# Attention scores in 24 units of one shape instead of 28 of three, with the products around them put in other places

## The reference

```python
    h = _L0_tok_ref(x, L0_tok_Wv, L0_tok_bv, L0_tok_Wo, L0_tok_bo, L0_tok_decay_w)
    h = h + _L0_attn_ref(_layernorm(h, axis=-1), L0_attn_wq, L0_attn_bq, L0_attn_wk, L0_attn_bk, L0_attn_wv, L0_attn_bv, L0_attn_wo, L0_attn_bo)
    h = h + _L0_ffn_ref(_layernorm(h, axis=-1), L0_ffn_router_w, L0_ffn_wg_r, L0_ffn_wu_r, L0_ffn_wd_r, L0_ffn_wg_s, L0_ffn_wu_s, L0_ffn_wd_s)
    return h
```

```python
        scores = jnp.einsum('bhqd,bhkd->bhqk', q, k) / jnp.sqrt(jnp.float32(hd))
        causal = jnp.tril(jnp.ones((s, s), dtype=bool))
        scores = jnp.where(causal, scores, -jnp.inf)
        weights = jax.nn.softmax(scores, axis=-1)
        attn = jnp.einsum('bhqk,bhkd->bhqd', weights, v)
```

## Time and profile before

| | |
|---|---|
| device time, median of 3 runs | 1868.26 us (1855.72 to 1869.14) |
| span of the profiled execution | 1852.8 us |
| lowest run over that span | 2.9 us |
| TensorE, VectorE, ScalarE, GpSimd busy | 1700.5, 1437.1, 976.7, 1056.0 us |
| a step of the attention phase | 34.09 us |

### The profile page before, as it was taken

The page is one execution under the profiler, slowest core; times in us unless marked ns, Lnnn a source line. Parts: engine busy times, 40 slices in busy tenths (PEclk is TensorE's granted clock), DMA queues, the critical chain, the costliest instruction groups (busy, mean ns, idle before and its releaser), DMA issues. The chain is left out here.

```text
span 1852.8 us, 49530 instructions
## 1 busy us (share of the span) xinstructions
PE 1700.5 (92%) x14718; PEld 1360.0 (73%) x14719; DVE 1437.1 (78%) x3985; ACT 976.7 (53%) x2048; POOL 1056.0 (57%) x1446
## 2 busy tenths in 40 slices
PE   5899999999999999999999998589999986988883
PEld 4677777777777777777777775368888876877773
DVE  4589899999999899899999996378888971455554
ACT  1166666666676666666666765333444422544441
POOL 4045555555555655655555556446777770567666
PEclk8899999999999999999999999679999997999996
DMA  2555556556556555555565453223333356999996
GB/s 76 80 132 152 141 128 158 142 119 166 141 135 144 147 147 138 135 154 142 123 162 141 123 147 99 109 74 105 126 120 120 122 155 169 286 327 326 323 331 220
DMA packets 226548, 291.13 MB, mean 157 GB/s; under 512 B 57142, under 2 KB 188954, under 8 KB 226458
## 3 DMA queue, kind: packets, MB, share of 16 engines
q1 hardware_dynamic: 190042, 186.14, 40.3%
q0 software_dynamic: 18048, 49.31, 8.2%
q10 hardware_dynamic: 18368, 54.64, 7.7%
HBM read 83.25 MB, written 129.69 MB: 115 GB/s over the span
## 5 line engine op out<-in xcount | busy, mean ns | idle before, releaser
L752 ACT ACTIVATE probs<-bank 128x376 f32<-128x376 f32 (+2 forms) x896 | 440.7, 529 | 272.9 <-PE bank L621 261.0
L843 DVE TENSOR_REDUCE neg_max<-bank 120x1 f32<-120x376 f32 (+2 forms) x896 | 507.0, 587 | 53.7 <-PE bank L587 49.7
L587 PE MATMUL bank<-k_rows,q_rows 64*128 64x128 f32 (+2 forms) x1536 | 403.7, 345 | 3.1 <-ACT probs L752 2.4
L621 PE MATMUL bank<-q_rows,k_rows 64*120 64x120 f32 (+2 forms) x1536 | 369.9, 336 | 3.9 <-ACT probs L752 3.6
L982 POOL TENSOR_SCALAR_AFFINE_SELECT probs<-probs 128x512 f32<-128x512 f32 (+1 forms) x384 | 232.4, 631 | 209.5 <-ACT probs L752 209.3
L604 PE MATMUL bank<-causal,own_row 56*120 56x56 bf16 (+4 forms) x1792 | 300.9, 248 | 8.7 <-DMA k_rows<-k_flat_hi 3.5
L587 PEld LDWEIGHTS bank<-k_rows,q_rows 64*128 64x128 f32 (+1 forms) x1536 | 246.2, 186 | 6.7 <-ACT probs L752 4.6
L2205 POOL DMA_INDIRECT y_got<-y_sorted,p_route x188 | 182.4, 970 | 119.7 <-issue 117.6
L621 PEld LDWEIGHTS bank<-q_rows,k_rows 64*128 64x128 f32 (+1 forms) x1536 | 229.8, 183 | 8.7 <-ACT probs L752 5.8
L604 PEld LDWEIGHTS bank<-causal,own_row 64*128 64x128 bf16 (+2 forms) x1792 | 153.4, 115 | 110.3 <-DVE neg_max L843 39.9
L1847 POOL DMA_INDIRECT x_sorted<-r_normed,route x188 | 184.3, 981 | 83.6 <-issue 59.0
(11 more groups left out here) (235 smaller groups left out, 4148.8 us busy)
## 6 DMA issues: line engine op xcount, KB each, us to landing
x_sorted<-zeros ACTq DMA_DIRECT2D x32, 816.0 KB, 3.8
y_sorted<-zeros ACTq DMA_DIRECT2D x32, 816.0 KB, 4.3
x_rows<-x_sorted SPq DMA_DIRECT2D x51, 512.0 KB, 6.4
y_sorted<-p_y_rows SPq DMA_DIRECT2D x51, 512.0 KB, 6.4
q_rows<-q_flat_hi SPq DMA_DIRECT2D x256, 94.0 KB
k_rows<-k_flat_hi SPq DMA_DIRECT2D x248, 94.0 KB
q_rows<-q_flat_lo SPq DMA_DIRECT2D x128, 94.0 KB
out_dram<-base SPq DMA_DIRECT2D x47, 256.0 KB, 5.0
```

The source lines that it names most:

```text
L587: last = eng.matmul(ps[0:T[t], m * w:(m + 1) * w], q[rows, slot, t * P:t * P + T[t]], k[rows, slot, 0:w], start=False, stop=(m == len(head ...
L621: last = eng.matmul(ps[0:T[t], m * w:(m + 1) * w], k[64 * c:64 * c + 64, slot, t * P:t * P + T[t]], q[64 * c:64 * c + 64, slot, t * P:S], ...
L752: eng.activation(probs[g % 2][0:T[t], first:first + len(heads), OFF[t]:OFF[t] + w], bank_exp[n % 2][0:T[t], 0:len(heads) * w].rearrange("k ...
L843: eng.tensor_reduce(dst, src, AX.X, ALU.max, negate=True).then_inc(max_taken, 1)
```

## The change

Each group has six units, so a step has 24. The first two (`PAIRS`) hold the second query tile of two heads each, for maxima and for exponents. The other four hold one head: for the maxima its third tile (376 keys) and behind it its first (128 keys), for the exponents its first (376 queries) and behind it its third (120). All banks are then nearly full, and all tiles are taken as 128 rows; for this `k_rows` is widened to 384 with zeros, and of `q_rows` the whole width is copied. A reduction of a one-head unit leaves four maxima, three of which belong to the third tile; `turn_maxima` joins these with one more reduction. `probs` is laid out anew (`OFF`), the masks come in the order second, first, third tile, and the first as well as the third wait for the group's last exponent.

What stands beside the units moves on all engines. TensorE: hid0 and hid1 after unit 1, value products of the last element's group 3 and val0 after 3, conv0 and conv1 after 7, nT after 9, value products of group 0 after 11, q0 and q1 after 13, k0 and k1 after 15, value products of group 1 and out0 after 17, those of group 2 and out1 after 21, val1 after 23. ScalarE's `keep` goes to units 4, 12, 18 and 22 (each behind that unit's exponent), the copies of conv to 7. SyncE's `load_x` moves to the head of the step.

The diff, cut to its core:

```diff
-    GROUPS, UNITS = 4, 7
+    GROUPS, UNITS = 4, 6
-    OFF = [0, CUT[0], CUT[0] + CUT[1]]
+    OFF = [0, CUT[0] + CUT[2], CUT[0]]
...
-        k_rows = [sb(f"k_rows{p}", [P, 8, S], F32R) for p in range(2)]
+        k_rows = [sb(f"k_rows{p}", [P, 8, SPAN], F32R) for p in range(2)]
...
-                return (["hid0", "hid1"] * front + ["val0"] * maxima
+                return (["hid0", "hid1"] * front + ["val0"] * maxima + ["conv0", "conv1"] * mix
                         + ["nT0", "nT1", "q0", "q1", "k0", "k1"] * front
-                        + ["out0", "out1"] * finish + ["conv0", "conv1"] * mix + ["val1"] * maxima)
+                        + ["out0", "out1"] * finish + ["val1"] * maxima)
...
+        PAIRS = 2
+        VALUES_AT = (3, 11, 17, 21)
 
         def max_bank(n):
 
-            return bank_max[1 if n == LAST_UNIT else n % 3]
+            return bank_max[n % 3]
...
+                    if u < PAIRS:
+                        slot, t, at = 4 * (g // 2) + 2 * u + m, 1, 2 * P * m
+                    else:
+                        slot, t, at = 4 * (g // 2) + u - PAIRS, (2, 0)[m], NT * P * m
+                    keys = min(S, (t + 1) * P)
+                    last = eng.matmul(ps[:, at:at + keys], q[rows, slot, t * P:(t + 1) * P], k[rows, slot, 0:keys],
+                                      start=False, stop=(m == 1), skip_group_check=True)
...
+                    if u < PAIRS:
+                        slot, t, at = 4 * (g // 2) + 2 * u + m, 1, CUT[1] * m
+                    else:
+                        slot, t, at = 4 * (g // 2) + u - PAIRS, (0, 2)[m], CUT[0] * m
+                    last = eng.matmul(ps[:, at:at + CUT[t]], k[64 * c:64 * c + 64, slot, t * P:(t + 1) * P],
                                       q[64 * c:64 * c + 64, slot, t * P:S],
+                                      start=(m == 0), stop=(m == 1), skip_group_check=True)
...
-                        if n in (1, 2) and st.front:
-                            hid_rows(st, n - 1)
-                        if u == 4:
+                        if n == 1 and st.front:
+                            hid_rows(st, 0)
+                            hid_rows(st, 1)
+                        if n in VALUES_AT:
+                            group = VALUES_AT.index(n) - 1
                             for t in range(NT):
-                                if g == 0 and st.finish:
+                                if group < 0 and st.finish:
                                     products_with_values(st, 3, -1, t)
-                                if g > 0 and st.attend:
-                                    products_with_values(st, g - 1, 0, t)
-                        if n == 7 and st.maxima:
+                                if group >= 0 and st.attend:
+                                    products_with_values(st, group, 0, t)
+                        if n == 3 and st.maxima:
                             values(st, 0)
+                        if n == 7 and st.mix:
+                            conv(st, 0)
+                            conv(st, 1)
...
-                        if n in (20, 22) and st.finish:
-                            out_rows_(st, (20, 22).index(n))
-                        if n in (24, 27) and st.mix:
-                            conv(st, (24, 27).index(n))
-                        if n == 27 and st.maxima:
+                        if n in (17, 21) and st.finish:
+                            out_rows_(st, (17, 21).index(n))
+                        if n == 23 and st.maxima:
                             values(st, 1)
...
+                    if u < PAIRS:
+                        dst = probs[g % 2][:, 2 * u:2 * u + 2, OFF[1]:OFF[1] + CUT[1]]
+                        src = bank_exp[n % 2][:, 0:2 * CUT[1]].rearrange("k (m w) -> k m w", m=2)
+                    else:
+                        dst = probs[g % 2][:, u - PAIRS, 0:CUT[0] + CUT[2]]
+                        src = bank_exp[n % 2][:, 0:CUT[0] + CUT[2]]
+                    eng.activation(dst, src, ACT.Exp).then_inc(exp_done, 1)
...
-                        if n == 5 and st.finish:
+                        if n == 4 and st.finish:
                             keep(st, 3, -1)
-                        if n == 7 and st.front:
+                        if n == 6 and st.front:
                             normalise(st)
...
+                        if st.mix and n == 7:
+                            for j in range(2):
+                                take_hi(st, f"conv{j}", mixed[0][:, j, :])
...
-                        if n in (11, 18) and st.attend:
-                            keep(st, (11, 18).index(n), 0)
+                        if n in (12, 18, 22) and st.attend:
+                            keep(st, (12, 18, 22).index(n), 0)
...
-                HALF_1_AT = {10: (0, 1), 12: (2,), 14: (3,), 16: (4,)}
-                HALF_0_AT = {21: (0,), 23: (1, 2), 25: (3,), 26: (4,)}
+                HALF_1_AT = {9: (0,), 11: (1,), 12: (2, 3), 13: (4,)}
+                HALF_0_AT = {20: (0,), 21: (1,), 22: (2, 3), 23: (4,)}
...
+                    if u < PAIRS:
+                        src = max_bank(n)[:, 0:4 * P].rearrange("q (m w) -> q m w", m=2)
+                        dst = neg_max[:, half, 4 * e + 2 * u:4 * e + 2 * u + 2, 4]
+                    else:
+                        src = max_bank(n)[:, 0:4 * P].rearrange("q (c w) -> q c w", c=4)
+                        dst = neg_max[:, half, 4 * e + u - PAIRS, 0:4]
                     eng.tensor_reduce(dst, src, AX.X, ALU.max, negate=True).then_inc(max_taken, 1)
...
+                    eng.tensor_reduce(neg_max[:, half, :, 5], neg_max[:, half, :, 0:3], AX.X, ALU.min).then_inc(max_joined, 1)
+                    eng.wait_ge(max_joined, done)
...
+                        if st.mix and n == 8:
+                            for j in range(2):
+                                take_lo(st, f"conv{j}", mixed[1][:, j, :], mixed[0][:, j, :])
...
-                    last_unit = (7, 3, 1)[t]
+                    last_unit = (UNITS, PAIRS, UNITS)[t]
...
-                            for t in reversed(range(NT)):
+                            for t in (1, 0, 2):
                                 mask(st, g, t)
...
                     if st.attend:
                         max_rows(st, 1, 0)
+                    if st.mix:
+                        load_x(st)
                     if isinstance(st.i, int) and st.real == B - 1:
...
                     if st.finish:
                         store(st)
-                    if st.mix:
-                        load_x(st)
```

More of the change, by code:

```diff
@@ L186, in attention_phase @@
         max_taken = sem("max_taken")
+        max_joined = sem("max_joined")
         max_hi = sem("max_hi")
@@ L595, in hide_later_keys @@
                     ps = max_bank(g * UNITS + u)
-                    t, heads = MAX_UNITS[u]
-                    w, d, m = KEYS_OF[t], T[t], len(heads)
                     rows = slice(64 * (g % 2), 64 * (g % 2) + 64)
+                    if u < PAIRS:
+                        blocks = ps[:, 0:4 * P].rearrange("q (m w) -> q m w", m=2)[:, :, P:2 * P]
+                    else:
+                        blocks = ps[:, 2 * P:4 * P].rearrange("q (m w) -> q m w", m=2)
                     for h in (1, 0):
[L601 to L604, removed]
+                        eng.matmul(blocks[:, :, 64 * h:P], own_row[rows, h, :], causal[rows, h, 0:2, 64 * h:P],
                                    start=(h == 1), stop=False, skip_group_check=True)
@@ L635, in scores @@
                         open_exp(st, g, u)
-                    for m in range(4):
-                        if st.maxima and m < len(MAX_UNITS[u][1]):
+                    for m in range(2):
+                        if st.maxima:
                             scores_for_max(st, g, u, m)
-                        if st.attend and m < len(EXP_UNITS[u][1]):
+                        if st.attend:
                             scores_for_exp(st, g, u, m)
@@ L800, in step @@
                                     eng.wait_ge(rows_loaded[(st.b + 1) % 2][h], st.turn(1, 208, 208))
-                        if st.front and n in (13, 15):
-                            j = (13, 15).index(n)
-                            take_hi(st, f"q{j}", q_flat[0][:, j, :], bias=bias_q[:, j:j + 1])
-                        if st.front and n == 17:
+                            for j in range(2):
+                                take_hi(st, f"q{j}", q_flat[0][:, j, :], bias=bias_q[:, j:j + 1])
+                        if st.front and n == 15:
                             for j in range(2):
                                 take_hi(st, f"k{j}", k_flat[0][:, j, :], bias=bias_k[:, j:j + 1])
-                        if st.mix and n in (25, 27):
-                            j = (25, 27).index(n)
-                            take_hi(st, f"conv{j}", mixed[0][:, j, :])
-                        if n == 25 and st.attend:
-                            keep(st, 2, 0)
                 run_steps(eng, step)
@@ L954, in step @@
```

(4 more changed lines are left out.)

112 lines of the change are left out of this document (43 added, 69 removed).

## The result

The changed kernel takes 2097.7 us (median of 4 runs, 2091.34 to 2104.16) against 1868.7 (1855.72 to 1869.77): 1.126 times as long, interval 1.121 to 1.131. The forecast was 1977, in a range up to 2045.

What follows compares the result with a forecast made beforehand. TensorE was taken to bound the step, VectorE 3 us behind. Own work 30.4 + long wait 4.1 + smaller waits 3.1 = 37.6 us against 34.1; thirty steps and two end steps add 109: 1977 us, range 1872 to 2045.

Steps and rivals of the forecast that it cites:

- The main wait: Group 2's value products wait for masks queued behind GpSimd's join and ScalarE's keep: 4.1 us in every step.
- (a) to (c): Smaller waits: unit 7 behind keep and exponents 1.35 us, transposes at unit 9 0.9, k behind q's bank 1.3.
- load_x costs nothing: At the head of SyncE's step, its wait for conv precedes that for q, so it holds nothing up.
- the clock: Rival: the clock falls in the new wait each step, value products cost 1.1 us more; 2036 us, chance 0.20.
- (a) to (d): All four smaller waits, the last being hid1 behind val1's late reading, 0.4 us; sum 3.95, taken at 3.1.
- half of the rest: Of the smaller waits, those for k and hid1 counted half, those at unit 7 and the transposes whole.
- Own work: TensorE's work per step without waits: 34.1 - 3.0 - 0.7 = 30.4 us, bounds 30.0 to 30.8.
- merged dense products: hid, conv and q each become one block and lose one tiling change on TensorE: 3 x 0.12 us.
- The ends of the phase: Two attention steps behind the thirty steady ones, without hid, q and k: some 2 us more each.
- long wait absent: Rival: group 2's masks come within TensorE's 3.2 us of work; step about 33.2 us, 1841 us, chance 0.08.
- Hidden, but only by the new wait: Transfers from q's second copy to next step's unit 0: 12.2 us of issues against 16 of TensorE, 11.9 without the wait.

Runs made afterwards that it cites:

- Masks ahead: Changed kernel with GpSimd's join of groups 0 and 1 behind the masks of group 2 instead of ahead of them: 1969.28 us, ratio 1.057.
- copy at 17: Changed kernel with ScalarE's copy (keep) of group 1 at unit 17 instead of unit 18: 1976.46 us, ratio 1.060.
- units only: Changed kernel's 24 units kept, everything between them unmerged and put back to about where it stood before the change: 1832.48 us, ratio 0.983.
- filler matmuls: Changed kernel plus twelve matmuls that nothing reads, between unit 21 and group 2's value products: 2032.01 us, ratio 1.089.
- both ends: Changed kernel with group 2's masks ahead of the join and group 1's copy at unit 17 together: 1997.8 us, ratio 1.069.

## Why the prediction was wrong

**Right.** The main wait, to a tenth: 4.1 walked, 4.22 found, with the walk's 7.3 us from the products of group 1 to those of group 2 measured at 7.54 (575.11 to 582.65). Masks ahead, copy at 17 and units only show the cause. It has two parts, though, only one of which the text named: by masks ahead, 2.84 hangs on the masks behind the join, and 1.38 stays in units 18 to 21 without it. Runs of two units without a wait take 0.91 to 0.92, as said. The signs and places of (a) to (c) are right too, and load_x costs nothing.

**The step that failed: the clock.** It was put aside as a rival at 0.20, though the text itself counted about 14 matmuls in 3.41 us of the new wait, fewer than the 18 in the stretch where the trace of before shows the fall. It came in every step. It was also priced too low: 1.1, for value products alone, as the earlier trace rows show them. The lower level lasts on through out1 and into units 22 and 23, and the rows make it 2.07; filler matmuls give back 2.1. By the Trainium skill (TensorE: Matmul & The Clock Gate, section Why this matters for your kernels), which the text cited, gaps between bursts send the clock down. The trace agrees, with 0.50 behind a stretch that had 0.49 us of work in 3.75.

**Terms that were mis-sized.** (a) to (d) were taken at 3.1, "half of the rest" on the argument that one wait covers another. The small waits measured are 1.39, 0.96, 1.14 and 0.38, 3.87 in sum, where the walks had said 1.35, 0.9, 1.3 and 0.4. (a) to (c) stand each at its own place, and none covered another. The fourth agrees by luck: hid1 has no wait for the reading of val1. The 0.38 stands ahead of unit 1, whose scores wait for the exponent of the last unit of the step before, and that stands in ScalarE's queue behind the copy of group 2. The same place one step on:

```profile
588.61 0.58 ACT L736 ACTIVATE attn_of_odd<-bank,strip_half 128x376 f32<-128x376 f32 x1
589.07 1.80 ACT L753 ACTIVATE probs<-bank 128x496 f32<-128x496 f32 x3
589.27 0.34 PE L597 MATMUL bank<-causal,own_row 64*128 64x128 bf16 x2
589.72 0.38 PE L616 MATMUL bank<-q_rows,k_rows 64*128 64x248 f32 x1
...
591.55 0.28 PE L507 MATMUL bank<-w_mix_hi,mixed_lo 128*128 128x256 f32 x1
591.66 0.28 PE L507 MATMUL bank<-w_mix_hi,mixed_hi 128*120 128x256 f32 x1
```

The first exponent of the three at 589.07 is the last unit's, 589.72 begins unit 1's scores, and 591.66 is hid1, right behind hid0.

Own work was taken at 30.4 and is 30.8, the upper bound: of the 0.7 for merged dense products and value products beside them 0.3 came. By the starts of the blocks the pairs gave their part: hid takes 2.32 for 1.61 + 0.90, q 2.27 for 1.23 + 1.23, conv 1.73 for 0.96 + 0.79. Value products beside a dense block gave nothing: they take 1.40, and val0 and out0 beside them 1.62 each, as before with scores between (1.40, 1.62, 1.61). By the Trainium skill (TensorEngine Tiling (Array Packing), section Key Properties) a change from one tiling mode to another drains the engine, and products with values beside a dense block still make one. That fits these starts, though no run here shows the drain itself. The sum: 37.6 forecast + 2.07 (clock) + 0.77 (waits) + 0.38 (own work) + 0.12 (the long wait) = 40.94.

**The ends of the phase.** The steps behind the steady ones were priced at +2 each. Those that begin at 1301.9 and 1340.6 take 38.7 and 37.7 against 31.2 and 29.0 before, with a mean clock of 0.84 and 0.69: they have the same wait, and with 301 and 220 matmuls instead of 336 less to keep TensorE at work. These ends and the start were +28 (22.5 + 5.3) where the text had +4.

**The rivals.** The clock's rival was the one that happened, and its 2036 was too low by the clock's price, own work and the ends. Of "long wait absent", 1841, no run shows the change itself, but units only comes to 1832 with no such wait. "Hidden, but only by the new wait", said of the transfers, is what masks ahead and both ends showed, and the zeros that ScalarE writes at the same time were not in the walk.

## What to carry to other kernels

Price a block of matmuls by what its neighbours hide, not by its own length: the new units were worth 1.2 us a step, and their neighbours' new places cost 8.1. A wait on TensorE that leaves few matmuls in it can have two prices, its length and the slower matmuls behind it; the second is read by filling the wait with matmuls that nobody needs. Waits walked one by one on different queues are to be added whole, unless the text can say which one covers which: (a) to (c) added up, while the transfers' wait stayed under the long one until that was cut.

## What was not expected of the hardware

In the change the lower clock level comes at the same place of each steady step, each time with about 6.8 us at 0.50 (539.48 to 546.31, 580.44 to 587.27). It begins in the wait, so that only the part behind the wait costs anything.

A write of 816 KB of zeros beside the small row transfers made two of SyncE's issues take 0.86 and 1.40 us in place of 0.59 and held rows of k back: steps of 36.8 where the clock stayed up and 38.3, often more, where it fell, against 35.5 with the write put seven units earlier.
